# A small GpSimd memset and a wait for it after every second payload scatter of a graph kernel

## The chip, the cores and the metric

The kernel runs on one core of a Trainium2 chip. The metric is the time in device microseconds of one execution; the runs shown are executions without a profiler, and the profile is one further execution with it.

## What is computed

A two-layer graph and expert network on 6250 nodes of 256 features. `src` and `dst` are 106250 edges, sorted by target in the input, and a second graph of 131072 edges belongs to the last layer. Cut to what matters here:

```
x = x + L0_gnn(layernorm(x))   # segment_sum of relu(edge_attr @ W_time) over src, two small products
x = x + L0_ffn(layernorm(x))   # router, top 2 of 6 experts, three dense layers each
x = x + L1_gnn(layernorm(x))   # two graph attention layers: softmax over the edges of each target
x = x + L1_ffn(layernorm(x))   # graph attention on 131072 edges gives the scores, top 2 of 4 experts
```

A node number is an index into 49 blocks of 128 nodes. The attention layers want their edges grouped by the block of the target, so the kernel first sorts the edges by block.

## The kernel before

`program` runs a row of stages, one after the other. Each stage is a block in which every engine has its own instruction stream, and all engines meet at its end before the next begins, so a stage lasts as long as its slowest engine. The first stage (`sorts`) computes for each edge the slot that it goes to. Three kinds of transfers are issued by GpSimd (POOL), one instruction for 128 rows: 832 scatters of edge attributes in `sorts` (line 274), 1856 payload scatters (line 449) and 3072 gathers of node rows in the three attention stages (line 790).

The payload scatters write four 32-bit words for each edge (`pay`: source node, target in its block, bits) to the slot that `pos` names in `pay_sorted`, a buffer in HBM that the attention stages load later. 832 belong to the first graph and 1024 to the second. They are not a stage of their own: the calls in `program` hand each earlier stage a share, which POOL works through while the other engines compute the stage. The shares in order: `edge_sums` 384, `norm_T` 56, `adapter` 148, `ln_stats` 24, `norm_T` 56, `router0` 56, `gates` 14, `experts` 94 and 560, `ln_stats` 24, `gat_tables` 104, `gat_tables` 104, `finish` 68, `ln_stats` 24, `norm_T` 56, `router_tables` 84. In these stages POOL does nothing else, and nobody waits for a single scatter; the end of the stage waits for all of them.

`scatter_pool` issues one share. It keeps two semaphores, `done[0]` and `done[1]`, which take turns every 16 scatters (`AHEAD`); before it begins a run of 16 it waits for the scatters of the same semaphore that were issued earlier, and at the end for all. `scatter_slots` makes the semaphores.

Of the kernel before, what the change touches and what calls it, by code (L numbers as in the profile page):

```python
# [23 lines left out]
P = 128  # L24
# [59 lines left out]
class Kernel:  # L84
# [54 lines left out]
    def setup(self, keep):  # L139
        self.keep = keep  # L140
        nc, i = self.nc, self.i
        ctx, sb, ps, sem = self.scope()

        def kp(name, shape, dt=F32):
            return keep.enter_context(nc.sbuf_tensor(name, shape, dt))

        self.X = kp("X", [P, NB, D])
        self.ident = kp("ident", [P, P])
        self.identb = kp("identb", [P, P], BF16)
        self.iota = kp("iota", [P, P])  # L150
        self.iotab = kp("iotab", [P, P], BF16)
        self.ones = kp("ones", [P, P])
        self.epsc = kp("epsc", [P, 1])
        self.rowid = kp("rowid", [P, 1])
        self.giota = kp("giota", [P, GC])
        self.mean = kp("mean", [P, NB])
        self.rstd = kp("rstd", [P, NB])
        self.grp = [kp(f"grp{g}", [1, n], I32) for g, n in enumerate(NGS)]
        self.pos = [None] + [kp(f"pos{g}", [P, n], I32) for g, n in ((1, ET), (2, FT))]
        self.pay = [None, kp("pay1", [P, ET, PW], I32), kp("pay2", [P, FT, PW], I32)]  # L160

        self.attr_sorted = nc.dram_tensor("attr_sorted", (NG0 * GE, ED + 1), F32).ap()
        self.pay_sorted = [None] + [nc.dram_tensor(f"pay_sorted{g}", (NGS[g] * KS[g] * P, PW), I32).ap() for g in (1, 2)]
        self.tab_gat = nc.dram_tensor("tab_gat", (PADROW + PADS, D + 3), F32).ap()
        self.tab_rt = nc.dram_tensor("tab_rt", (PADROW + PADS, RT), F32).ap()
        s_o, s_st = sem("s_const"), sem("s_zero")
        self.s_x = keep.enter_context(nc.semaphore("s_x"))
        with ctx, nc.Block() as block:
            @block.vector
            def _(dve):  # L170
                c = Chain(dve, s_o)
                c(nc.vector.memset(self.X[:, NB - 1, :], 0.0))
                nc.vector.memset(self.ones[:, :], 1.0)
                nc.vector.memset(self.epsc[:, :], EPS)

            @block.gpsimd
            def _(pool):
                pool.iota(self.iota[:, :], [[1, P]], base=0, channel_multiplier=0,
                          allow_small_or_imprecise_dtypes=True)
                pool.iota(self.iotab[:, :], [[1, P]], base=0, channel_multiplier=0,  # L180
                          allow_small_or_imprecise_dtypes=True)
                pool.iota(self.rowid[:, :], [[1, 1]], base=0, channel_multiplier=1,
                          allow_small_or_imprecise_dtypes=True)
                pool.iota(self.giota[:, :], [[P, GC]], base=0, channel_multiplier=1,
                          allow_small_or_imprecise_dtypes=True)
                for m in (self.ident, self.identb):
                    pool.memset(m[:, :], 0.0).then_inc(s_st, 1)
                pool.wait_ge(s_st, 2)
                for m in (self.ident, self.identb):
                    pool.affine_select(out=m[:, :], in_=m[:, :], compare_op=ALU.not_equal, fill=1.0, base=0,  # L190
                                       pattern=[[-1, P]], channel_multiplier=1)
# [240 lines left out]

    def scatter_slots(self, sem, g, lo, hi):

        return dict(g=g, lo=lo, hi=hi, done=sem.pool(2))

    def scatter_pool(self, pool, s):

        g, lo, hi, done = s["g"], s["lo"], s["hi"], s["done"]  # L440
        out = self.pay_sorted[g]
        last = pool.to_reg(out.shape[0] - 1)
        issued = [0, 0]
        for n in range(hi - lo):
            j = n // AHEAD % 2
            if n % AHEAD == 0 and issued[j]:
                pool.wait_ge(done[j], 16 * issued[j])
            issued[j] += 1
            pool.indirect_dma_start(  # L449
                out=out, out_offset=bass.IndirectOffsetOnAxis(ap=self.pos[g][:, lo + n:lo + n + 1], axis=0),  # L450
                in_=self.pay[g][:, lo + n, :], in_offset=None,
                bounds_check=last, oob_is_err=False).then_inc(done[j], 16)
        for j in range(2):
            if issued[j]:
                pool.wait_ge(done[j], 16 * issued[j])
# [1841 lines left out]
```

## Time and profile before

| | us |
|---|---|
| median of 2 runs | 8330.28 (8316.3 to 8344.27) |
| span of the profiled execution | 10342.3 |
| POOL busy in it | 5780.8 (56%), 5760 of its 5781 instructions are indirect DMAs |
| PE busy | 5494.0 (53%) |
| DVE busy | 5413.1 (52%) |
| ACT busy | 3566.1 (34%) |

The profiled execution took 2012 us longer than the median without the profiler. In the rows, a time at the start of a line is in us from the start of the span. PE is TensorE, PEld its weight loads, DVE is VectorE, ACT is ScalarE, POOL is GpSimd. A bracket such as [0.30 <-issue] is the idle time of the engine before the instruction and what ended it; "issue" means that it waited for nothing that the profile shows, and "remote" that a semaphore changed whose updater the profile could not tell. The duration on an indirect DMA's row is POOL's own work on it, not the landing of the data.

### The profile page before, as it was taken

To read this page: it belongs to the slowest core of one execution; us is meant where nothing else is said; L and a number is where in the kernel's file an instruction comes from. 1 tells how busy PE (TensorE), PEld (TensorE's weight loads), DVE (VectorE), ACT (ScalarE), POOL (GpSimd) and SP (SyncE) were. 2 spreads that over 40 slices of the span, in tenths; PEclk is the share of its full clock that TensorE was granted. 3 is DMA by queue.
4 is the path that set the end of the run, shared out by engine and by line. 5 is a ranking of instruction groups with operands and counts; after the bars stand their busy time and mean duration, and the time that the engine had idled before them with its cause. 6 is when DMAs were issued, how large, how long until landed. Compare 5 with 4: busy or idle time off the path is not lost. (4 is left out here: it accounts for less than half of the span.)

```text
span 10342.3 us, 116779 instructions
## 1 busy us (share of the span) xinstructions
PE 5494.0 (53%) x22610; PEld 3209.3 (31%) x22610; DVE 5413.1 (52%) x18917; ACT 3566.1 (34%) x11436; POOL 5780.8 (56%) x5781
## 2 busy tenths in 40 slices
PE   0000001593221149936777764777771388888897
PEld 0000000481110025523444432444441134434445
DVE  8577400492200012226666654666663287788777
ACT  0000000241000012214666642666661176666662
POOL 3787767307567740044666654666666566566650
PEclk9999975795565569967878876888885577677658
DMA  4111100010000000002333321333330111111113
GB/s 128 24 21 22 23 11 4 22 40 3 2 23 1 1 1 0 0 12 84 91 91 91 92 64 57 92 91 91 92 89 2 25 23 22 23 23 24 22 22 101
DMA packets 476242, 426.24 MB, mean 41 GB/s; under 512 B 269726, under 2 KB 409876, under 8 KB 475668
## 3 DMA queue, kind: packets, MB, share of 16 engines
q0 software_dynamic: 214016, 282.62, 11.8%
q1 hardware_dynamic: 224020, 120.13, 4.3%
q10 hardware_dynamic: 37632, 17.48, 0.7%
q8 instruction: 159, 2.61, 0.1%
q14 instruction: 415, 3.40, 0.1%
HBM read 341.50 MB, written 78.72 MB: 41 GB/s over the span
## 5 line engine op out<-in xcount | busy, mean ns | idle before, releaser
L449 POOL DMA_INDIRECT pay_sorted<-pay,pos x1856 | 1883.4, 1015 | 1893.7 <-PEq L1217 721.2
L790 POOL DMA_INDIRECT G<-tab_gat,pay x1856 | 1770.4, 954 | 1187.3 <-issue 465.5
L790 POOL DMA_INDIRECT G<-tab_rt,pay x1216 | 1151.5, 947 | 816.0 <-PE pLU L867 353.0
L864 PE MATMUL pU<-G,PM 128*128 128x257 f32 x3712 | 1269.6, 475 | 324.3 <-ACT PM L961 191.4
L274 POOL DMA_INDIRECT attr_sorted<-rows,pos x832 | 972.9, 1169 | 411.3 <-issue 253.4
L864 PEld LDWEIGHTS pU<-G,PM 128*128 128x128 f32 x3712 | 808.2, 241 | 485.4 <-ACT PM L961 235.6
L1679 DVE TENSOR_TENSOR t<-pO,BL 128x1024 f32<-128x1024 f32 (+1 forms) x78 | 90.7, 1163 | 1345.3 <-remote 871.0
L1078 DVE TENSOR_REDUCE mt<-pW 128x4 f32<-128x2048 f32 x304 | 695.4, 2287 | 163.5 <-issue 77.6
L810 PE MATMUL pA<-identb,G 128*20 128x128 bf16 (+1 forms) x3072 | 438.6, 250 | 477.8 <-issue 202.8
L1663 ACT ACTIVATE H<-pH,B 128x512 f32<-128x512 f32 (+1 forms) x312 | 206.6, 663 | 1364.6 <-remote 691.2
L909 ACT ACTIVATE aT<-pA 20x256 bf16<-20x256 bf16 (+1 forms) x1232 | 512.3, 416 | 457.1 <-PE pA L810 170.5
L1626 PE MATMUL pO<-WL,H 128*128 128x256 f32 x1176 | 288.8, 401 | 573.6 <-issue 345.7
L1167 DVE SCALAR_TENSOR_TENSOR e<-e 128x256 f32<-128x256 f32 x928 | 396.2, 427 | 366.8 <-ACT e L955 292.8
L955 ACT ACTIVATE e<-pW,adst 128x256 f32<-128x256 f32 x928 | 438.0, 472 | 298.8 <-DVE mt L1051 209.4
L961 ACT ACTIVATE PM<-pP 128x256 f32<-128x256 f32 x928 | 339.6, 366 | 574.0 <-PE pP L836 380.6
L810 PEld LDWEIGHTS pA<-identb,G 128*20 128x20 bf16 (+1 forms) x3072 | 190.2, 98 | 1081.4 <-issue 1064.6
L836 PE MATMUL pP<-ident,PT 128*128 128x128 f32 x1856 | 490.6, 354 | 0.0
L1051 DVE TENSOR_REDUCE mt<-pW 128x1 f32<-128x256 f32 x928 | 389.6, 420 | 189.5 <-PE pW L820 136.9
L1175 DVE SCALAR_TENSOR_TENSOR acc<-acc,alpha,pU 128x257 f32 x928 | 442.5, 477 | 77.8 <-PE pU L864 41.2
L970 ACT ACTIVATE PT<-e,bias 128x256 f32<-128x256 f32 x928 | 458.3, 494 | 0.7 <-DVE e L1167 0.7
L322 ACT ACTIVATE rows<-lo 128x16 f32<-128x16 f32 x52 | 11.6, 229 | 1291.8 <-DMA attr_sorted<-rows,pos 1223.4
L593 PE MATMUL pT<-ident,attr 128*128 128x128 f32 x256 | 76.0, 297 | 708.5 <-issue 674.4
(324 smaller groups left out, 12213.3 us busy)
## 6 DMA issues: line engine op xcount, KB each, us to landing
pay_sorted<-pay,pos POOLq DMA_INDIRECT x1856
G<-tab_gat,pay POOLq DMA_INDIRECT x1856
G<-tab_rt,pay POOLq DMA_INDIRECT x1216
expert_parts<-pos SPq DMA_DIRECT2D x144, 128.0 KB
yl<-expert_parts SPq DMA_DIRECT2D x36, 512.0 KB, 4.0
attr_sorted<-zattr SPq DMA_DIRECT2D x1, 16896.0 KB, 53.2
rows<-attr_sorted ACTq DMA_DIRECT2D x256, 66.0 KB
attr_sorted<-rows,pos POOLq DMA_INDIRECT x832
```

What stands on the lines that cost most here:

```text
L274: pool.indirect_dma_start(out=self.attr_sorted, out_offset=bass.IndirectOffsetOnAxis(ap=pos0[:, t:t + 1], axis=0), in_=rows[:, j, k, :], i ...
L449: pool.indirect_dma_start(out=out, out_offset=bass.IndirectOffsetOnAxis(ap=self.pos[g][:, lo + n:lo + n + 1], axis=0), in_=self.pay[g][:, ...
L790: pool.indirect_dma_start(out=G[:, j, k, 0:R], out_offset=None, in_=table, in_offset=bass.IndirectOffsetOnAxis(ap=pay[:, g % (2 * PART), k ...
L810: ins = nc.tensor.transpose(pA[j % len(pA)][:, k * P:(k + 1) * P], parts[:, k, 0:ROWS], self.identb[:, :])
L836: ins = nc.tensor.transpose(pP[j % 2][:, k * P:(k + 1) * P], PT[:, j % 2, k * P:(k + 1) * P], self.ident[:, :])
L864: ins = nc.tensor.matmul(u[:, 0:F], PM[:, j % 2, k * P:(k + 1) * P], G[:, j, k, 0:F], start=(k == 0), stop=(k == K - 1))
L909: a.activation(aT[:, j % 2, :], pA[j % len(pA)][:, 0:K * P], ACT.Copy).then_inc(s_aT, 1)
L955: a.activation(e[:, j % 2, :], pW[j % 2][:, 0:K * P], ACT.Identity, bias=ad).then_inc(s_y, 1)
L970: a.activation(PT[:, s, :], e[:, s, :], ACT.Exp, bias=bias[:, j % 4:j % 4 + 1]).then_inc(s_PT, 1)
L1078: v.tensor_reduce(mt, pW[:, :, :], AX.X, ALU.max).then_inc(s_max, 1)
L1167: v.scalar_tensor_tensor(e[:, j % 2, :], e[:, j % 2, :], SLOPE, e[:, j % 2, :], ALU.mult, ALU.max).then_inc(s_e, 1)
L1175: v.scalar_tensor_tensor(ac, ac, alpha[:, j, 0:1], pU[j % 2][:, 0:F], ALU.mult, ALU.add).then_inc(s_acc, 1)
```

## The change

A constant tile `idle` of 128 x 128 f32 is added in SBUF, and each share gets one more semaphore, `s_idle`. After each scatter with an odd number in its share POOL clears the tile, and waits for the clear before it goes on to the next scatter. Every share is even, so there are 1856 / 2 = 928 such clears and waits. Nothing reads the tile.

```diff
@@ setup @@
         self.rowid = kp("rowid", [P, 1])
+        self.idle = kp("idle", [P, P])
@@ scatter_slots @@
-        return dict(g=g, lo=lo, hi=hi, done=sem.pool(2))
+        return dict(g=g, lo=lo, hi=hi, done=sem.pool(2), idle=sem(f"s_idle{g}_{lo}"))
@@ scatter_pool @@
-        g, lo, hi, done = s["g"], s["lo"], s["hi"], s["done"]
+        g, lo, hi, done, idle = s["g"], s["lo"], s["hi"], s["done"], s["idle"]
@@ the loop over the scatters of a share, behind the scatter @@
                 bounds_check=last, oob_is_err=False).then_inc(done[j], 16)
+            if n % 2:
+                pool.memset(self.idle[:, :], 0.0).then_inc(idle, 1)
+                pool.wait_ge(idle, n // 2 + 1)
```

## Rows read from the trace of the kernel before

**Rows 1.** Windows of two stages: us, PE, PEld, DVE, ACT, POOL busy (x), PEclk, DMA, GB/s
```profile
1413.00:1924.00 511.00, 59.55 (x205) 46.93 (x205) 35.98 (x143) 13.05 (x38) 383.26 (x384) 0.52 0.04 6
1924.00:2310.00 386.00, 354.68 (x2611) 329.91 (x2611) 336.50 (x1652) 164.03 (x474) 0.46 (x1) 0.95 0.17 40
2888.00:3778.00 890.00, 162.16 (x344) 86.34 (x344) 26.71 (x46) 28.86 (x42) 675.63 (x654) 0.58 0.05 8
3778.00:4451.00 673.00, 648.56 (x2080) 389.16 (x2080) 187.48 (x327) 177.74 (x270) 0.19 (x1) 0.98 0.00 0
```

**Rows 2.** Timeline of PE and ACT in experts: with scatters, and (last row) behind them
```profile
2934.07 3.60 PE L1615 MATMUL pH<-XT,W 128*128 128x512 f32 x8
...
2982.29 0.69 ACT L1663 ACTIVATE H<-pH,B 128x512 f32<-128x512 f32 x1 [51.81 <-remote]
2993.48 0.69 ACT L1663 ACTIVATE H<-pH,B 128x512 f32<-128x512 f32 x1 [10.50 <-remote]
...
3809.99 0.69 ACT L1663 ACTIVATE H<-pH,B 128x512 f32<-128x512 f32 x1 [0.97 <-PE pH L1615]
```

**Rows 3.** Timeline of DVE in sorts, two instructions behind DVE's own work
```profile
900.46 0.49 DVE L356 TENSOR_SCALAR mask<-hi,iota 128x1024 bf16<-128x1024 bf16 x1 [1.38 <-issue]
903.08 2.36 DVE L357 TENSOR_TENSOR_SCAN rank<-mask,base,zero 128x1024 f32<-128x1024 bf16 x1 [2.13 <-issue]
```

**Rows 4.** Line 449 alone: duration ns min/median/max, first and last start
```profile
L449 POOL DMA_INDIRECT pay_sorted<-pay,pos x1856: 969/974/12956, 1413.6 to 8122.1; - x186
```

**Rows 5.** Timeline of POOL and DVE, last scatter of ln_stats and start of the next stage
```profile
2668.51 0.97 POOL L449 DMA_INDIRECT pay_sorted<-pay,pos  x1 [0.30 <-issue]
...
2673.56 2.71 DVE L1263 TENSOR_SCALAR xn<-X,mean,rstd 128x256 f32<-128x256 f32 x8 [16.46 <-PEq L127]
```

**Rows 6.** Windows: POOL's share of sorts, and the stage behind the last gather
```profile
161.00:1388.00 1227.00, 7.77 (x32) 4.38 (x32) 736.77 (x921) 12.57 (x50) 972.70 (x832) 1.00 0.12 22
...
10123.00:10342.00 219.00, 182.22 (x672) 123.57 (x672) 157.41 (x288) 58.47 (x87) 0.00 (x0) 0.91 0.37 118
```

**Rows 7.** Groups of the page: gathers, xcount, busy us, mean ns, idle us before
```profile
L790 POOL DMA_INDIRECT G<-tab_gat,pay x1856 | 1770.4, 954 | 1187.3 <-issue 465.5
L790 POOL DMA_INDIRECT G<-tab_rt,pay x1216 | 1151.5, 947 | 816.0 <-PE pLU L867 353.0
```

**Rows 8.** Timeline of DVE in attention, the same step of two groups in a row
```profile
5000.06 0.42 DVE L1051 TENSOR_REDUCE mt<-pW 128x1 f32<-128x256 f32 x1
...
5002.39 0.42 DVE L1051 TENSOR_REDUCE mt<-pW 128x1 f32<-128x256 f32 x1
```

**Rows 9.** Windows of norm_T, adapter and gat_tables: the stage, and behind its scatters
```profile
2311.00:2399.00 88.00, 19.64 (x98) 16.70 (x98) 17.49 (x49) 13.27 (x26) 54.53 (x56) 0.57 0.02 2
...
2383.00:2399.00 16.00, 6.00 (x34) 5.11 (x34) 5.85 (x17) 6.75 (x14) 0.28 (x1) 0.66 0.00 0
...
2399.00:2638.00 239.00, 111.53 (x225) 47.31 (x225) 71.25 (x140) 24.48 (x39) 153.92 (x148) 0.60 0.03 3
...
2600.00:2638.00 38.00, 22.82 (x45) 9.80 (x45) 14.92 (x29) 4.91 (x9) 0.01 (x1) 0.54 0.00 0
...
4487.00:4720.00 233.00, 78.05 (x294) 62.12 (x294) 80.17 (x350) 25.62 (x39) 101.82 (x104) 0.65 0.11 32
...
4620.00:4720.00 100.00, 56.23 (x214) 44.50 (x214) 61.31 (x273) 19.29 (x30) 0.43 (x1) 0.74 0.15 54
```

**Rows 10.** Timeline of POOL at its start: a memset, a wait for it, the first indirect DMA
```profile
1.56 0.20 POOL L187 MEMSET identb<- 128x128 bf16 x1
1.92 0.29 POOL L190 TENSOR_SCALAR_AFFINE_SELECT ident<-ident 128x128 f32<-128x128 f32 x1 [0.17 <-POOL identb L187]
...
161.93 2.26 POOL L274 DMA_INDIRECT attr_sorted<-rows,pos  x1 [157.89 <-DVE pos L401]
```

**Rows 11.** Timeline of PE and POOL: a gather that waited for PE
```profile
8715.63 0.36 PE L867 MATMUL pLU<-pfs,pay 128*128 128x60 bf16 x4
...
8716.26 0.95 POOL L790 DMA_INDIRECT G<-tab_rt,pay  x1 [2.91 <-PE pLU L867]
```

## The prediction

> **What bounds the kernel now.** I read the windows stage by stage first, then the timelines inside the two longest stages with scatters, then POOL's rows alone. In the profiled execution, a stage that carries scatters falls into two halves. In `edge_sums` PE finishes 205 matmuls in the 511 us in which POOL scatters, and 2611 in the 386 us behind them; in `experts` it is 344 in 890 us against 2080 in 673 us [rows 1]. So the profile shows scatters and compute nearly one after the other.
>
> I do not believe that this is so without the profiler. In `experts` the matmuls that feed ACT start at 2934.07 and last 3.60 us by their rows, yet ACT comes by them at 2982.29, and by the next after another 11.2 us; behind the scatters the same gap is 0.97 us [rows 2]. And DVE in `sorts`, behind instructions of its own that were done, sits for 1.38 and 2.13 us on nothing that the profile shows [rows 3]. Engines that stop without a wait while small records of all of them are written out look like a cost of being profiled. The Trainium skill says of the notification block ("NOTIFIC — the notification-queue block", section 7.1) that its internal pipeline holds the producers back rather than lose a record; no run here shows that block itself.
>
> The times say the same. POOL does its indirect DMAs strictly one behind the other. A payload scatter takes 0.974 us [rows 4] with 0.30 us in front of it [rows 5], so 1.279 us from start to start, and a gather 0.95 + 0.30 = 1.25 us [rows 7]. POOL's whole line of work is then: until the end of the attribute scatters 1388 us [rows 6], 1856 x 1.279 = 2374 us, 3072 x 1.25 = 3840 us, and 219 us behind the last gather [rows 6]. That is 7821 us, against a span of 10342.3 and a median of 8330.28. The median leaves only 509 us in which POOL can stand still. If scatters and compute were serial there too, the tails of two stages alone (386 + 673 us, rows 1) would break that sum. So either POOL is the bound of nearly the whole unprofiled run, or it is quicker without the profiler.
>
> Whether compute would be long enough to hide POOL, I take from the stretches without scatters, scaled by PE's matmuls [rows 1, 9]:
> - `edge_sums`, with 2611 + 205 = 2816 matmuls: 2816 x 386 / 2611 = 416 us, against 384 x 1.279 = 491 us of scatters.
> - `experts`, with 2080 + 344 = 2424 matmuls: 2424 x 673 / 2080 = 784 us, and the loading of its weights ahead of that, against 654 x 1.279 = 836 us.
> - `norm_T`: 98 x 16 / 34 = 46 us, against 72 us (three times).
> - `adapter`: 225 x 38 / 45 = 190 us, against 189 us.
> - `gat_tables`: 294 x 100 / 214 = 137 us, against 133 us (twice).
> - `ln_stats` waits for POOL even in the profile: the last scatter starts at 2668.51, and DVE, idle for 16.46 us, goes on at 2673.56 [rows 5].
> - `router0`, `gates`, `finish` and `router_tables` have 222 scatters together; I take them as bound by POOL too.
> In attention a group of two gathers costs POOL 2.5 us, and DVE, where nothing stops it, needs 2.33 us [rows 8]. So POOL is the longest engine, or level with it, everywhere.
>
> **What the change costs.** It removes nothing and moves nothing: 928 memsets and 928 waits come in on POOL, and the following scatter cannot be launched before the wait ends. Nobody else waits for the tile. Behind the waiting instruction stand the remaining scatters of the share, and behind those the end of the stage for all engines.
>
> A pair of scatters today is 2 x 1.279 = 2.558 us. In the new pair one gap of 0.305 us is replaced by: the time from a scatter's end to the memset's start, the memset, and the time from its completion to the start of the next scatter. The trace of before has no memset behind an indirect DMA, so I bound this.
> - Memset: 0.20 us, the row of a 128x128 one [rows 10].
> - Completion to next start: after the wait for that memset the next instruction starts 0.17 us later by the idle before it [rows 10]. A gather that waited for PE starts at 8716.26, 0.27 us after the matmul's end at 8715.99 [rows 11]. The gather is the nearer one: 0.27.
> - Scatter's end to memset: between nothing and the 0.305 us that stands in front of every scatter.
> Low end: 0 + 0.20 + 0.27 - 0.305 = 0.165 us a pair. High end: 0.305 + 0.20 + 0.305 - 0.305 = 0.505 us, where the launch behind the wait is as dear as any other. I take 0.31, about the middle: I see no row that says how much of the 0.305 us the memset would have to sit through.
>
 It also advises to time POOL by the spacing of starts and not by the durations; the rows agree that the two differ, 1.279 against 0.974.
>
> Sum: 928 x 0.31 = 288 us. Off it goes the slack of `gat_tables`, 4 us in one of its two stages with the rates above: 284 us. The bounds give 928 x 0.165 = 153 us and 928 x 0.505 = 469 us. The new semaphores and the tile lie outside POOL's line and I cost them at nothing; one semaphore more to clear at a stage's end would be far below 1 us in each of the 15 stages.
>
> Against the medians that is 8330 + 284 = 8614 us. In the profiled execution, whose own time is 10342.3 us, the same 928 pauses lie on POOL, but if the other engines make up held-back work in them, little or nothing of the 284 us shows: I expect its span between 10340 and 10630 us. The medians stand 2012 us below the span, so I do not carry a ratio over, I add the pauses.
>
> **Rivals.**
> - *POOL is quicker without the profiler* (1.0 us instead of 1.279). Then `edge_sums` has 32 us of slack, `experts` 130, `adapter` 42 and the `gat_tables` 33 each. At 0.31 us the pauses fit into the last three; 28 us of `edge_sums` stay, and the small stages with 462 scatters or 231 pauses, 72 us: together 100 us, 8430 us. For it: the 2012 us must come from somewhere. Against it: POOL's line falls to 7821 - 5760 x 0.28 = 6208 us, and some 2120 us would have to be waits of POOL that the stretches above do not hold.
> - *The serial halves are real.* Then compute goes on at full pace in the pauses, each us of pause saves one behind the scatters, and it ends near 8330 us. For it: [rows 1] as they stand. Against it: the 7821 us sum.
> - *Faster.* As above, but held-back PE and DVE work passes at each change of POOL's instruction. A third instruction for every two scatters would let half as much again through: 172 more matmuls in `experts` at 0.32 us and 103 in `edge_sums` at 0.15 us, 71 us, and with the smaller stages about 100 us, 8230 us. It needs two and a half times the present rate, not one and a half, to be worth over 2%.
> - *Switching is dear.* The first indirect DMA after the memsets took 2.26 us against 0.974 [rows 10]. If each change of instruction kind costs those 1.29 us again, the pause is 1.6 us and the time 8330 + 928 x 1.6 = 9815 us. Against it: that was the first of all, beside DVE at work, and a gather behind an idle time of 2.91 us took 0.95 [rows 11]. The Trainium skill ("GPSIMD Engine Reference", 2.1) has a load of about 6 us on the first call of a freshly loaded kernel; nothing in these rows shows it repeated.
>
> **How the numbers follow.** My forecast, pauses in full on the path, gets 62%; POOL quicker 13%; serial halves 15%; faster 4%; dear switching 6%. About 2%, 167 us, is what a measurement of this kernel tells from no change. In the forecast a pause of 0.18 us suffices for that, and I give its low end 5 of the 62. So slower is 57 + 3 (POOL a little quicker, dearer pauses) + 6 = 66%; within 2% is 5 + 10 + 15 = 30%; faster 4%. The range reaches from 8340, which leaves out most of the serial and the faster cases, to 8810, a little over the high end of the sum (8330 + 469 = 8799). The forecast's own range is 8480 to 8800.
>
> **What would show it.** In the changed kernel's profile: between the starts of scatters 1.279 us inside a pair and 1.44 to 1.78 us across a memset; memset rows of about 0.2 us; `ln_stats`, 12 pauses, longer by 2 to 6 us, since POOL bounds it there already. If `edge_sums` ends no later although its last scatter does, pauses are filled by the other engines. Medians within 100 us of 8330 would say that compute hides or fills the pauses; a memset row or a wait above 0.5 us would say that I mis-sized the pause; medians below 8200 would mean that scatters hold the other engines back on the chip itself.

## The result and the profile after

The changed kernel takes 8480.56 us (median of 2 runs, 8438.7 to 8522.42) against 8330.28, a ratio of 1.0188 with a 95% interval of 1.0099 to 1.0276. Timed again with more runs it is 8504.92 us (6 runs) against 8322.96 (17 runs of before), a ratio of 1.0226 [1.0201, 1.0252]: slower, by 182 us. A ratio is the record's own figure with its interval, not the quotient of the two medians, and differs from that a little. By the first two runs alone it stays open whether the change reaches 2%. I forecast 284 us more, with 153 to 469 us as the ends.

The profiled execution of the changed kernel spans 8436.9 us, and not the 10340 to 10630 us that I expected. It is one of the two timed runs, the one of 8438.7 us; so it is with all nine traces taken after the forecast, each of which is one of the timed runs of its kernel. For these, "executions without a profiler" in the section on the metric does not hold. The trace of before belongs to none: no timed run took 10342.3 us. A second profiled execution of the unchanged kernel spans 8348.1 us, inside the range of its other timed runs (8303.33 to 8360.64). So the 10342.3 us behind the rows of before were a disturbed execution, of which nothing recurs in the nine other traces. I call these two the second trace of before and the trace of after, and compare these.

The page of after, its span and the engines' busy times:
```profile
span 8436.9 us, 117816 instructions
...
PE 4991.5 (59%) x22610; PEld 2989.4 (35%) x22610; DVE 5410.9 (64%) x18917; ACT 3602.3 (43%) x11436; POOL 5971.7 (71%) x6709
```
POOL has 928 instructions more than the 5781 of before. The other engines have done the same work.

The windows of `edge_sums` and of `experts` (us, PE, PEld, DVE, ACT, POOL busy, PEclk, DMA, GB/s), each cut where the compute ends, second trace of before:
```profile
1402.00:1805.00 403.00, 380.39 (x2816) 352.70 (x2816) 376.10 (x1795) 177.16 (x512) 305.17 (x308) 1.00 0.21 45
1805.00:1905.00 100.00, 0.00 (x0) 0.00 (x0) 0.00 (x0) 0.00 (x0) 74.01 (x76) 0.51 0.03 2
2411.00:3199.00 788.00, 761.32 (x2424) 453.62 (x2424) 214.16 (x372) 206.58 (x312) 594.16 (x604) 0.98 0.05 9
3199.00:3266.00 67.00, 0.00 (x0) 0.00 (x0) 0.00 (x0) 0.00 (x0) 49.39 (x51) 0.50 0.03 1
```
And the same in the trace of after:
```profile
1402.00:1805.00 403.00, 379.74 (x2816) 351.84 (x2816) 374.53 (x1793) 176.89 (x512) 316.79 (x431) 1.00 0.21 45
1805.00:1940.00 135.00, 0.00 (x0) 0.00 (x0) 0.00 (x0) 0.00 (x0) 104.57 (x146) 0.50 0.02 2
2476.00:3265.00 789.00, 762.72 (x2424) 454.11 (x2424) 214.21 (x372) 206.61 (x312) 616.49 (x844) 0.98 0.05 9
3265.00:3392.00 127.00, 0.00 (x0) 0.00 (x0) 0.00 (x0) 0.00 (x0) 99.05 (x138) 0.51 0.02 1
```
Three things stand in these rows. First, all 2816 matmuls of `edge_sums` and all 2424 of `experts` run beside the scatters; the halves of [rows 1] are gone, in both kernels. Second, in the last part of each stage PE, DVE and ACT do nothing at all: only scatters are left, so POOL ends the stage. Third, the compute keeps its length under the change (403 and 788 to 789 us) and only the tail with POOL alone grows, from 100 to 135 us and from 67 to 127 us.

The timeline of POOL in after, at the start of `edge_sums`, answers to [rows 5] and shows one pause:
```profile
1403.33 0.97 POOL L450 DMA_INDIRECT pay_sorted<-pay,pos  x1 [0.30 <-issue]
1404.28 0.24 POOL L455 MEMSET idle<- 128x128 f32 x1
1404.80 0.97 POOL L450 DMA_INDIRECT pay_sorted<-pay,pos  x1 [0.28 <-POOL idle L455]
1406.07 0.97 POOL L450 DMA_INDIRECT pay_sorted<-pay,pos  x1 [0.30 <-issue]
1407.03 0.23 POOL L455 MEMSET idle<- 128x128 f32 x1
1407.54 0.97 POOL L450 DMA_INDIRECT pay_sorted<-pay,pos  x1 [0.28 <-POOL idle L455]
```
The clear starts where the scatter ends (1403.33 + 0.97 = 1404.30 against 1404.28), takes 0.24 us, and the next scatter starts 0.28 us after it. From a scatter behind a clear to the next such one it is 1407.54 - 1404.80 = 2.74 us, against 2 x 1.278 in the second trace of before, whose rows are 1.278 us apart:
```profile
1405.52 0.97 POOL L449 DMA_INDIRECT pay_sorted<-pay,pos  x1 [0.30 <-issue]
1406.80 0.97 POOL L449 DMA_INDIRECT pay_sorted<-pay,pos  x1 [0.30 <-issue]
1408.08 0.97 POOL L449 DMA_INDIRECT pay_sorted<-pay,pos  x1 [0.31 <-issue]
```
So a pause is 0.18 us here.

The groups of POOL in after, which answer to [rows 4, 7] (group, xcount, busy us, mean ns, idle us before them and what ended it):
```profile
L450 POOL DMA_INDIRECT pay_sorted<-pay,pos x1856 | 1853.2, 998 | 668.2 <-issue 292.1 <-POOL idle L455 253.0 <-POOLq L127 43.7
...
L794 POOL DMA_INDIRECT G<-tab_rt,pay x1216 | 1150.4, 946 | 544.8 <-issue 288.4 <-PE pLU L871 245.0 <-DMA pay<-pay_sorted 11.4
...
L455 POOL MEMSET idle<- 128x128 f32 x928 | 224.6, 242 | 0.0
```
The 928 clears had no idle time ahead of them. 16 of them stand behind the last scatter of a share, so 912 lie between two scatters, and these took 912 x 0.242 = 221 us. The scatters behind them waited 253.0 us, where the same launches would have stood 912 x 0.305 = 278 us. 221 + 253 - 278 = 196 us. Two small amounts come off it: by their rows the clears start a little before the scatter ahead of them ends, 13 us in all, and line 450's mean duration is 5 ns shorter than in the second trace of before (998 against 1003), 9 us over 1856. That leaves 174 us. Added up from the first start to the last end in each of the 16 shares, scatters take 2433.8 us in the second trace of before and 2606.3 in after: 172.5 us, or 0.186 us for each of the 928 pauses.

The spans differ by less, 8436.9 - 8348.1 = 88.8 us. The rest is the last attention stage, which went from 1786.4 us to 1713.9 in these two executions, 72.5 us the other way. There POOL's gathers wait for PE, 245.0 us of it in the row above, and 313.8 in the second trace of before; PE's mean granted clock in that stage was 0.75 in after against 0.70. In the repeat of the changed kernel (below) it was 0.72, and the stage took 1758.2 us. Which of its two levels PE is granted there differs from execution to execution, and no row ties it to the change. Such a difference is enough to explain why the two first runs of the changed kernel lie 84 us apart, though the slower of them has no trace to show it by; the record has its mean granted clock over the whole run, 0.828 against 0.841.

### The profile page after: what moved, and what is told of

It is laid out like the page before. It is cut to its first block and busy times, and to the rows that moved or that the text cites. A ratio compares the mean times of both kernels' runs of the same rounds, so it can differ in the third digit from the quotient of the medians.

```text
span 8436.9 us, 117816 instructions
## 1 busy us (share of the span) xinstructions
PE 4991.5 (59%) x22610; PEld 2989.4 (35%) x22610; DVE 5410.9 (64%) x18917; ACT 3602.3 (43%) x11436; POOL 5971.7 (71%) x6709
## 5 line engine op out<-in xcount | busy, mean ns | idle before, releaser
L450 POOL DMA_INDIRECT pay_sorted<-pay,pos x1856 | 1853.2, 998 | 668.2 <-issue 292.1
L868 PE MATMUL pU<-G,PM 128*128 128x257 f32 x3712 | 1096.7, 423 | 2.5 <-DVE acc L1179 2.5
L814 PE MATMUL pA<-identb,G 128*20 128x128 bf16 (+1 forms) x3072 | 418.7, 240 | 599.5 <-DMA G<-tab_gat,pay 519.0
L868 PEld LDWEIGHTS pU<-G,PM 128*128 128x128 f32 x3712 | 719.8, 216 | 73.5 <-ACT PM L965 2.9
L840 PE MATMUL pP<-ident,PT 128*128 128x128 f32 x1856 | 451.3, 329 | 0.0
L893 PE MATMUL pE<-W,pay 128*128 128x256 f32 x1152 | 445.3, 555 | 0.0
L832 PE MATMUL pW<-aT,sel 28*128 28x512 bf16 x1216 | 381.8, 441 | 12.3 <-DVE mt L1082 12.3
```

Source lines behind the costliest of these rows:

```text
L450: pool.indirect_dma_start(out=out, out_offset=bass.IndirectOffsetOnAxis(ap=self.pos[g][:, lo + n:lo + n + 1], axis=0), in_=self.pay[g][:, ...
L814: ins = nc.tensor.transpose(pA[j % len(pA)][:, k * P:(k + 1) * P], parts[:, k, 0:ROWS], self.identb[:, :])
L840: ins = nc.tensor.transpose(pP[j % 2][:, k * P:(k + 1) * P], PT[:, j % 2, k * P:(k + 1) * P], self.ident[:, :])
L868: ins = nc.tensor.matmul(u[:, 0:F], PM[:, j % 2, k * P:(k + 1) * P], G[:, j, k, 0:F], start=(k == 0), stop=(k == K - 1))
L893: ins = nc.tensor.matmul(pE[:, 0:D], hid[u % 2][:, k, i * P:(i + 1) * P], W2[:, x, k, :], start=(k == 0), stop=(k == HID // P - 1))
```

## The experiments

**The kernel before, again.** No edit.

> The kernel before, unchanged, once more. If the 10342 us span of its first profile was a disturbance of that one execution, the new profile has a span within 30 us of its timed runs (about 8330), compute and scatters overlap in it, and in edge_sums and experts the scatters end last (384 x 1.279 = 491 us and 654 x 1.279 = 836 us). If the serial halves belong to this kernel whenever it is profiled, the span is near 10340 again. Ratio to the kernel before: 1.000, and the width of its interval is what no change at all can show.

Measured: 8322.91 us (10 runs), ratio 0.9992 [0.997, 1.0015], and a span of 8348.1 us with the windows shown above. The serial halves, the stalls in front of ACT [rows 2] and those of DVE [rows 3] are not there. In the second trace the same two instructions, counted by their place in the loop, come 0.44 us and 0.11 us behind the one before, where [rows 3] have 1.38 and 2.13 us. No instruction of line 357 waits more than 0.13 us there.
```profile
724.95 0.49 DVE L356 TENSOR_SCALAR mask<-hi,iota 128x1024 bf16<-128x1024 bf16 x1 [0.44 <-DVE posf L365]
725.55 2.36 DVE L357 TENSOR_TENSOR_SCAN rank<-mask,base,zero 128x1024 f32<-128x1024 bf16 x1
```
It gives the lengths that I had to scale out of the disturbed rows. In each stage with scatters, the last scatter ends behind the last instruction of PE, DVE and ACT:

| stage | compute ends | last scatter ends | POOL alone |
|---|---|---|---|
| edge_sums | 1805.0 | 1903.4 | 98.4 |
| norm_T (first) | 1931.5 | 1982.4 | 50.9 |
| adapter | 2164.5 | 2193.0 | 28.5 |
| router0 | 2369.1 | 2384.4 | 15.3 |
| gates | 2402.8 | 2410.1 | 7.3 |
| experts | 3198.3 | 3263.6 | 65.3 |
| gat_tables (first) | 3427.9 | 3449.2 | 21.3 |
| gat_tables (second) | 4779.1 | 4794.2 | 15.1 |
| finish | 6037.4 | 6099.7 | 62.3 |
| router_tables | 6290.6 | 6330.6 | 40.0 |

The five shares that are not in the table end alone as well: the three of `ln_stats` by 12.4 us each, the other two of `norm_T` by 50.9 and 50.6. No stage can hide a pause on POOL, neither the two in which I saw compute level with it nor any other.

**The changed kernel, again.** The diff is the change's own.

> The changed kernel, unchanged, in five rounds. POOL's line as the bound: 928 pauses of 0.19 us (pairs of 2.74 us in its profile against 2.56 before), 176 us, ratio 1.021. If other engines take back part of the pauses: 1.00 to 1.015.

Measured: 8504.92 us, ratio 1.0226 [1.0201, 1.0252], span 8487.5. The shares take 2605.7 us, 172.0 more than in the second trace of before, the same as in after to 0.5 us. The pauses are thus steady, and what differs between executions lies elsewhere.

**A clear and a wait after every scatter.**
```diff
-            if n % 2:
-                pool.memset(self.idle[:, :], 0.0).then_inc(idle, 1)
-                pool.wait_ge(idle, n // 2 + 1)
+            pool.memset(self.idle[:, :], 0.0).then_inc(idle, 1)
+            pool.wait_ge(idle, n + 1)
```

> The clear and the wait after every scatter, 1856 of them. POOL's line as the bound: 1856 x 0.19 = 353 us, ratio 1.042. If the cost of the change is no matter of the pauses (the tile, the semaphores, a drift between runs): the same as the changed kernel, about 1.02. If compute hides the first part of it: more than twice the cost of the changed kernel.

Measured: 8692.04 us, ratio 1.0431 [1.0398, 1.0464], 369 us over before. The shares take 2782.8 us, 349.1 more, which over 1856 pauses is 0.188 us each. Twice the pauses cost twice the time, with nothing hidden and nothing dearer, as the timeline of POOL shows, one clear to each scatter:
```profile
1421.91 0.23 POOL L454 MEMSET idle<- 128x128 f32 x1
1422.42 0.97 POOL L450 DMA_INDIRECT pay_sorted<-pay,pos  x1 [0.28 <-POOL idle L454]
1423.38 0.22 POOL L454 MEMSET idle<- 128x128 f32 x1
```

**The wait moved ahead of the next clear.** POOL still does every clear, but the scatter behind it no longer waits.
```diff
             if n % 2:
+                if n > 1:
+                    pool.wait_ge(idle, n // 2)
                 pool.memset(self.idle[:, :], 0.0).then_inc(idle, 1)
-                pool.wait_ge(idle, n // 2 + 1)
+        pool.wait_ge(idle, (hi - lo) // 2)
```

> The same 928 clears, but each wait stands ahead of the next clear, two scatters later, where the clear has long ended. If it is the wait for the completion that costs (the next scatter is launched only behind it), the launch runs beside the clear and 0 to 0.05 us of each pause stay: ratio 1.000 to 1.006. If it is the clear itself that costs, 0.2 us on GpSimd: ratio 1.02 as with the wait.

Measured: 8409.54 us, ratio 1.0113 [1.008, 1.0146]. The shares take 2506.9 us, 73.2 more, or 0.079 us a pause. That lies between the two cases expected, 0 to 0.05 and about 0.2 us, and is neither. Timeline of POOL:
```profile
1419.34 0.97 POOL L450 DMA_INDIRECT pay_sorted<-pay,pos  x1 [0.30 <-issue]
1420.30 0.23 POOL L457 MEMSET idle<- 128x128 f32 x1
1420.69 0.97 POOL L450 DMA_INDIRECT pay_sorted<-pay,pos  x1 [0.17 <-issue]
```
The clear is where it was and as long as it was. The scatter behind it comes 0.17 us after the clear's end and not 0.28. So of the 0.186 us of a pause, 0.107 are due to the wait being for this clear, and 0.079 remain without: about two thirds of the clear's 0.242 us then pass within the gap that stands ahead of a scatter anyway.

That a memset not waited for costs less than its row is long can be seen without scatters too. In the second trace of before, POOL starts with these two memsets of one column, 0.02 us apart, though their rows are 0.10 and 0.11 us long:
```profile
0.26 0.10 POOL L2286 MEMSET const-float32-0.0<- 128x1 f32 x1 [0.26 <-issue]
0.28 0.11 POOL L2286 MEMSET const-float32-1.0<- 128x1 f32 x1
```

**A clear of one column.** Same wait, 128 x 1 elements and not 128 x 128.
```diff
-                pool.memset(self.idle[:, :], 0.0).then_inc(idle, 1)
+                pool.memset(self.idle[:, 0:1], 0.0).then_inc(idle, 1)
```

> As the change, but each clear writes one column of the tile (128 x 1) and not all 128. Theory: POOL is the bound of every scatter stage, and a pause is the clear's own duration + the launch behind the wait (0.28 us) - the gap that stood there (0.305 us). With a clear of about 0.06 to 0.12 us in place of 0.235 the pause is 0.04 to 0.10 us: 928 x that = 35 to 90 us, ratio 1.004 to 1.011. Rival, the price lies in the change of instruction kind whatever the clear does: 0.187 us a pause as in the change, ratio about 1.022.

Measured: 8413.9 us, ratio 1.0113 [1.0065, 1.0161]; the shares take 2510.3 us, 76.5 more, or 0.082 us a pause. Group and timeline of POOL:
```profile
L455 POOL MEMSET idle<- 128x1 f32 x928 | 127.1, 137 | 0.0
```
```profile
1422.93 0.12 POOL L455 MEMSET idle<- 128x1 f32 x1
1423.33 0.97 POOL L450 DMA_INDIRECT pay_sorted<-pay,pos  x1 [0.28 <-POOL idle L455]
```
A clear of a 128th of the elements still takes 0.137 us on average, 57% of the 0.242 of the whole tile, so my 0.06 to 0.12 us was too low. The launch behind the wait is again 0.28 us. The clear became 0.242 - 0.137 = 0.105 us shorter and the pause 0.186 - 0.082 = 0.104 us. The pause follows the clear's duration; it is no fixed price of changing from one kind of instruction to another.

**The wait without a clear.** POOL's own stream raises the semaphore.
```diff
-                pool.memset(self.idle[:, :], 0.0).then_inc(idle, 1)
+                pool.sem_inc(idle, 1)
                 pool.wait_ge(idle, n // 2 + 1)
```

> No clear: after every second scatter POOL raises the semaphore itself and waits for it. Theory: the wait is for nothing that POOL works on, so the next scatter's launch is only put off by two small instructions of its stream: 0 to 0.1 us a pair, 0 to 90 us, ratio 1.000 to 1.011. Rival, the wait alone breaks the run of scatters and is most of the pause: 0.187 us a pair, ratio about 1.022.

Measured: 8322.08 us, ratio 0.9991 [0.9966, 1.0017]. The shares take 2431.8 us, 2.0 less than in the second trace of before. Timeline of POOL:
```profile
1421.04 0.97 POOL L450 DMA_INDIRECT pay_sorted<-pay,pos  x1 [0.30 <-issue]
1422.31 0.97 POOL L450 DMA_INDIRECT pay_sorted<-pay,pos  x1 [0.30 <-POOLq L455]
1423.59 0.97 POOL L450 DMA_INDIRECT pay_sorted<-pay,pos  x1 [0.30 <-issue]
```
The gap in front of a scatter with the two instructions ahead of it is the same 0.30 us as in front of one without, only its releaser is named differently. 928 increments and 928 waits that find their value are free here; in the changed kernel the wait cost time because the launch of the next scatter had to begin behind the clear.

**Pauses in `experts` alone.** A flag limits the change's lines to the two shares of that stage.
```diff
-            if n % 2:
+            if n % 2 and self.pauses:
```

> The change's clear and wait, but in the two shares of the stage experts only: 654 scatters, 327 pauses. Theory: the stage ends with its last scatter, compute 65 us ahead of it, so every pause counts: 327 x 0.187 = 61 us, ratio 1.007. Rival, compute hides a part of them: the stage no longer than before, ratio 1.000.

Measured: 8394.18 us, ratio 1.0073 [1.0033, 1.0112], which is 61 us of 8337.01. The window of the stage behind its compute, which in before is 67 us long:
```profile
2411.00:3199.00 788.00, 762.18 (x2424) 453.93 (x2424) 214.17 (x372) 206.56 (x312) 616.83 (x844) 0.98 0.05 9
3199.00:3326.00 127.00, 0.00 (x0) 0.00 (x0) 0.00 (x0) 0.00 (x0) 98.49 (x137) 0.50 0.02 1
```
Compute ends at 3197.4 as in before (3198.3), and the last scatter at 3323.8 and not 3263.6, although the first starts 1.5 us earlier than there. All 327 pauses are on the path: the two shares take 61.6 us more in the trace, 0.188 us a pause.

**Clears where POOL has nothing to do.** No pauses among the scatters, and 360 clears, each with its wait, in the last stage.
```diff
+        @block.gpsimd
+        def _(pool):
+            for n in range(360):
+                pool.memset(self.idle[:, :], 0.0).then_inc(s_idle, 1)
+                pool.wait_ge(s_idle, n + 1)
```

> No clear among the scatters; instead POOL does 360 clears, each with its wait, in the last stage, where it has nothing else to do. Theory: a clear costs only POOL's own time, so nothing is delayed: ratio 1.000 (within 0.003), last stage 215 us as before. Rival, the clears take something from the other engines (SBUF access beside DVE and the loads): the last stage longer by 20 us or more, ratio 1.0025 or more.

Measured: 8331.01 us, ratio 1.0005 [0.9982, 1.0027]. The group of the clears, and the window of the stage:
```profile
L2048 POOL MEMSET idle<- 128x128 f32 x360 | 73.9, 205 | 50.8 <-POOLq L127 30.1
```
```profile
8108.00:8322.00 214.00, 181.62 (x672) 123.38 (x672) 157.47 (x288) 58.48 (x87) 73.93 (x360) 0.92 0.37 119
```
The stage takes 213.3 us, against 214.5 in before (8108.1 to 8321.4, against 8128.6 to 8343.1), and DVE is busy for 157.47 us in it, against 157.49 in the same stage of the second trace of before. In this stage the clears take nothing from anyone but POOL that could be measured. They also show what a clear and its wait cost when the next one is a clear again: they were over in 94 us, 0.26 us each.

The runs together, by what the shares take in the trace (2433.8 us without pauses; for experts alone, of its two shares) and by the timed ratio:

| kernel | pauses | added in the trace | a pause | ratio |
|---|---|---|---|---|
| change | 928 | 172.5 and 172.0 | 0.186 and 0.185 | 1.0226 |
| every scatter | 1856 | 349.1 | 0.188 | 1.0431 |
| late wait | 928 | 73.2 | 0.079 | 1.0113 |
| one column | 928 | 76.5 | 0.082 | 1.0113 |
| wait without clear | 928 | -2.0 | 0 | 0.9991 |
| experts alone | 327 | 61.6 | 0.188 | 1.0073 |
| clears elsewhere | 0 | | | 1.0005 |

No variant is quicker than the kernel before, and none could be expected to be, since all of them only add to POOL.

## Why the prediction was right, and where it was not

**The direction and the mechanism were right.** Pauses on POOL lie on the path that ends each stage with scatters, in full. The table of stages shows it for before, the tails of 135 and 127 us for after, and the run with pauses in `experts` alone prices a single stage as the sum would: 327 x 0.188 us.

**The doubt about the serial halves was right, the reason given for it half so.** I would not take [rows 1] at their word, because [rows 2, 3] had engines that stopped without a wait, and because POOL's line of 7821 us left no room in 8330. Both pointed the right way: without the disturbance the compute runs beside the scatters. But I called it "a cost of being profiled", and nine other profiled executions, the second of the unchanged kernel among them, have none of it, and each of them is one of the timed runs. It was that one execution. What disturbed it is not settled: no run here brought it back.

One thing in its trace I overlooked. Most of its records of semaphore changes are missing: it holds 51,436 of them, and the second trace of before 134,404, with the same 116,779 instructions in both. The page shows it in the issues of the scatters, which have no time to landing in the first trace (first row) and one of 2.1 us in the second:
```profile
pay_sorted<-pay,pos POOLq DMA_INDIRECT x1856
pay_sorted<-pay,pos POOLq DMA_INDIRECT x1856, 2.1
```
So the labels "issue" and "remote" in [rows 2, 3] say little about what an engine waited for; that it stopped for longer than in the other traces stands. The recording itself was thus part of the disturbance. Whether it slowed the engines, or both have another cause, no run shows. From the disturbance also follows the one number that failed outright, a span of 10340 to 10630 us for the changed kernel. I carried a one-time disturbance over as if it belonged to the kernel.

The Trainium skill ("NOTIFIC — the notification-queue block", section 7.1), which I cited for producers being held back rather than a record being lost, does not say that this happens in each profile. The nine undisturbed traces show no engine held back like this, and in the disturbed one records are missing as well; where they were lost no run shows.

**The step that was mis-sized is the pause, and in it one term.** Of the three terms, the launch behind the wait was 0.28 us (taken 0.27, from the gather of [rows 11]), and the clear 0.242 (taken 0.20, from [rows 10]). The type is not the reason: the f32 memset of 128 x 128 in the same trace took 0.196, and clears that follow one another take 0.205, so the rest goes with the place behind a scatter. The third, from the scatter's end to the clear's start, I let go from 0 to 0.305 us, and took about the middle. It is 0 by the rows: the clears of after have 0.0 us of idle time before them in all 928 cases. Were a clear's own time the 0.205 us that it takes among its like, 0.02 us would be left for the third term, of the 0.228 us from a scatter's end to the clear's end. The 0.305 us in front of a scatter is not a time that POOL needs after a scatter, but one that it needs ahead of an indirect DMA. With that, the sum is 0 + 0.242 + 0.28 - 0.305 = 0.217 us by the terms, and 0.186 by the shares, where the overlap and the shorter scatters told of above are in it. That is near my low end of 0.165, and 928 x 0.186 = 173 us, where I had 288. The rule on the DSPs that I set against my choice (the Trainium skill, "Perfetto Trace Analysis", GPSIMD Engine Instruction; that two of them write the descriptors stands there under DMA Instruction — SWDGE (GPSIMD)) put the sum at the low end, and by that the measurement sides with it; that a part of the DSPs begins early is not what a trace here can show.

The semaphore more in each share, which I costed at nothing, is small as I said. Between the last scatter of a share and the first of the next stage's it took 0.03 to 0.17 us more in after than in the second trace of before, outside attention, and as much in the run without clears.

Could I have seen it? [rows 10] hold the hint: the AFFINE_SELECT behind the memset started 0.17 us after its wait, and a gather 0.27 us after its own [rows 11], which points to the kind of instruction that comes next, and not the one that was, as what sets the gap; the two waits had different engines to wait for, so it is a hint and no more. I used both rows for the second term and did not ask what they say on the first.

**The slack of the stages.** I took 4 us off for a `gat_tables` stage whose compute I had longer than its scatters (137 against 133 us), and saw `adapter` level. In the second trace of before POOL ends behind the compute by 21, 15 and 28 us there. The error of 4 us hides in the rest, but the way to it was poor: rates out of the disturbed rows made compute look longer than it is (norm_T 46 us by the rates, 21 in the trace).

**"POOL is the longest engine, or level with it, everywhere"** does not hold for the last attention stage. This is the row of its gathers in the second trace of before:
```profile
L790 POOL DMA_INDIRECT G<-tab_rt,pay x1216 | 1153.1, 948 | 614.7 <-PE pLU L867 313.8 <-issue 289.3 <-DMA pay<-pay_sorted 11.6
```
About half of the idle time before the gathers is a wait for PE. The change adds nothing in that stage, so the sum did not suffer; a change that quickens POOL's gathers there would have been mispriced.

**The rivals.** *POOL is quicker without the profiler* falls: the nine executions with a trace are themselves among the timed runs, and in the second trace of before scatters are still 1.28 us apart. *Serial halves* falls with the windows. *Faster*, by held-back work that passes in the pauses, falls with them, as there is no such work. *Switching is dear* falls: the scatters behind a clear take 0.97 us, and a clear of one column lowers the price. `ln_stats`, where I expected 2 to 6 us, grew from 30.4 us (2199.2 to 2229.5) to 32.4 (2250.3 to 2282.8). One figure of the prediction is wrong by its own terms: for *Faster*, half as much again was worth 100 us, so the 167 us of 2% need about 1.8 times the present rate and not two and a half; no result hangs on it.

**The range.** Both medians, 8480.56 and 8504.92, lie in it, at the low edge of the likeliest case's own 8480 to 8800, since the pause lies near the low end of its bounds. That the first of them lies inside this edge by 0.56 us is luck: it is the middle of two runs 84 us apart, and its 150 us over before lie under my low end of 153, and are about half of the 284. The 2% that I asked for "slower" needed a pause of 0.18 us, and 0.186 is as near to it as can be; that this low end got 5 of 62 in my chances was too little.

## What to carry to other kernels

Where the same small work is issued a thousand times on the engine that ends each stage, price the gap and not only the instruction: find out whether the idle time belongs to the instruction in front of it or to the one behind, since new work fits into the second at a part of its duration. A wait costs if the launch of the next instruction has to begin behind it; here, taking it one turn later removed more than half of the price. And where the profiled span stands far from the timed runs, treat the profile as another execution, take durations of single instructions from it, and let neither its stage lengths nor its span enter a forecast. If its DMA issues lack a time to landing that another trace of the kernel gives for them, records are missing, and its reasons for waits are not to be relied on either.

## What the runs showed of the hardware

- An indirect DMA on POOL starts 0.28 us after the end of a memset that it waits for, 0.30 us after another indirect DMA, and 0.17 us after a memset that it doesn't wait for; the memset starts at the end of the indirect DMA, without a gap.
- A memset of 128 x 1 f32 took 0.137 us and one of 128 x 128 0.242 us on average among the scatters, and 0.205 us among its like. Two of one column that nothing waited for started 0.02 us apart.
- An increment and a wait in POOL's own stream, 928 times, cost nothing that can be measured (ratio 0.9991 [0.9966, 1.0017]).
- In stretches without a matmul the granted clock stands at 0.50 to 0.51, the lower level of 1.2 GHz. In the last attention stage, with the same 6901 matmuls in each, it was a mixture of both levels that differs from execution to execution. Here are the windows of that stage in the second trace of before and, behind it, in the trace of after:
```profile
6339.00:8127.00 1788.00, 1567.23 (x6901) 752.07 (x6901) 1512.18 (x6439) 1282.97 (x3742) 1153.07 (x1216) 0.70 0.14 26
```
```profile
6502.00:8217.00 1715.00, 1469.60 (x6901) 733.97 (x6901) 1505.38 (x6439) 1278.44 (x3742) 1150.36 (x1216) 0.75 0.16 27
```
PE is busy 98 us longer at a mean clock of 0.70 than at 0.75, and the stage is 73 us longer. Over all nine undisturbed traces the stage takes 1714 to 1786 us. Runs of one kernel lie up to 80 us apart (8297.42 to 8377.14 among 21 of before), and I take this stage to be the largest part of it; the timed runs without a trace have no stage times to show it by. Their mean clock over the whole run goes with it: 0.831 in the two slowest of the 21, 0.845 in the quickest. What decides the level in one execution and not in another is open.
